# Graph layers over 25,000 edges: the last group's indirect transfers name 106 partitions instead of 128

## The chip, the core and the metric

The kernel is one program on one core of a Trainium2 chip. The metric is the device time of one launch in microseconds: the median of several executions. The core has a tensor engine (PE), a vector engine (DVE), a scalar engine (ACT), a GpSimd engine (POOL), and SyncE (SP), which here only issues transfers; transfers themselves run on 16 DMA engines.

## What is computed

The input is a table `x` of 50,000 nodes by 96 features, 25,000 edges (`src`, `dst`, sorted by `dst`), 17 attributes for each edge, and small weights. Four graph layers follow one another, each with a residual sum and a layer norm:

```python
x = _layernorm(x + _L0_gnn_ref(x, edge_index, edge_attr_17, ...))   # messages weighted by a small network
x = _layernorm(x + _L1_gnn_ref(x, edge_index))    # 10 times: out = spmm(out) * 0.9 + x * 0.1
x = _layernorm(x + _L2_gnn_ref(x, edge_index))    # 16 times: h = 0.9 * segment_sum(norm * h[row], col) + 0.1 * x
x = _layernorm(x + _L3_gnn_ref(x, edge_index, ...))  # two graph convolutions with weights and prelu
```

Each of the 10 + 16 + 2 steps after layer 0 gathers one row of 96 floats for every edge, adds the rows of edges that share a target node, and writes the sums for the next step.

## The kernel before, in words

**Tiles and groups.** The edges are laid out in 49 groups (`NGP`) of 512 slots: partition p of a group holds four consecutive slots (`U = 4`), and for each of the four there is one indirect transfer with one index for each partition, 128 rows of 384 bytes. So a pass over all edges is 49 x 4 = 196 indirect transfers, all issued by POOL. 48 groups (`GF`) are full. The last group holds 25,000 - 48 x 512 = 424 edges, which is exactly 106 partitions x 4; its partitions 106 to 127 are padding, with an index that is clamped into the table for a gather and out of bounds for a scatter.

**Stages.** The set-up (layer 0, histograms, ranks of the edges; not touched by the change) is followed by `passes()`, called four times: `power` (layer 1, 10 passes), `smooth` (layer 2, 16 passes), `conv1` and `conv2` (layer 3, one pass each). In a pass, for each group: POOL gathers four tiles into one of seven buffers `G` (line 1924), PE transposes them into a PSUM bank (1956), DVE scans along the sorted edges with a mask (2129), PE turns the result back (1976 or 1985), DVE combines it with the group's own rows (2154, 2169), and SP stores the result into the table of the next pass (2374). In `power` and `smooth` PE turns back group n two steps late: at the step of group 48, the last, it first turns back 46 and 47 and only then transposes 48 (`backs`, lines 1724 to 1728, and the loop at 2014).

**Order on POOL.** POOL issues in program order. It starts group g when group g-2 has landed (1920 to 1922) and the buffer is free. It starts a new pass when all stores of the pass before have landed (1912, 1913). Between the last gather of a pass and that wait other indirect transfers stand: in `power` 23 gathers of the nodes' own rows (1907; 12 in the last pass), in `smooth` a "lot" of two or three groups of finished rows that are scattered to the output (`send_lots`, 1881: 8 transfers in 10 passes, 12 in the five after them, 24 behind the last pass). In front of the `smooth` passes stand 196 gathers of own rows (1894). In `conv2` scatters of finished groups to the output (`send`, 1856) alternate with gathers, and the last twelve groups are scattered at the end. In 22 passes three of the four tiles of group 45 (`ROW_GROUP`) are fetched row by row by SP and ACT instead (1819); that is no part of the change.

**The last group.** It takes four indirect transfers in each place: 10 passes of `power`, the own rows of `power` (1907), the own rows of `smooth` (1894), 16 passes of `smooth`, the gathers of `conv1` and `conv2`, the last lot (1881, in `conv1`), and the last scatter (1856): 32 places, 128 transfers.

Of the kernel before, what the change touches and what calls it, by code (L numbers as in the profile page):

```python
# [19 lines left out]
N, E, D, ED = 50000, 25000, 96, 17  # L20
P = 128
U = 4
# [4 lines left out]
GF = E // GE  # L27
# [13 lines left out]
RG = 7  # L41
# [19 lines left out]
LOT_LOADED = {"smooth": tuple((p, 42) for p in range(15)) + ((15, 12), (15, 24)), "conv1": ((0, 8), (0, 20))}  # L61
ROW_GROUP, ROW_TILES, ROW_FROM, ROW_LOAD = NGP - 4, 3, 2, 8
ROWS = P * ROW_TILES
ROW_SHARES = {"sp": (0, 120, 3), "act": (120, ROWS, 7)}
EPS = 1e-5
GD = U * D
# [17 lines left out]
def slots_of(flat):  # L84

    return flat.rearrange("(g p u) -> p g u", p=P, u=U)


def by_group(x):
# [29 lines left out]
class Tail:  # L119


    def __init__(self, prog, s):
# [13 lines left out]
        def tmp(n, shape):  # L136
            return s.enter_context(nc.sbuf_tensor(f"tail_{n}", shape, fp32))

        self.X = tmp("x", [P, GD])
        wide = tmp("xt0", [D + 2, GE])  # L140
        prog.row_index = wide[D:D + 2, 0:ROWS].bitcast(i32)
        self.xt = [wide[0:D, :], tmp("xt1", [D, GE])[:, :]]
# [281 lines left out]
class Program:  # L424
# [50 lines left out]
    def build(self):  # L475
# [46 lines left out]
        self.outc = self.dram("outc", [TR, D])  # L522
        self.index_rows = self.dram("index_rows", [4, ROWS], i32)

# [773 lines left out]
    def prepare(self):  # L1298
# [4 lines left out]
        with ExitStack() as s:  # L1303
# [78 lines left out]
            def _(sp):  # L1382
# [14 lines left out]
                def order_out():  # L1397

                    sp.wait_ge(linked, 1)
                    with nc.allow_non_contiguous_dma(reason="four numbers of each partition"):  # L1400
                        sp.dma_start(slots_of(self.mask_s[1:TR + 1]), by_group(cont[:, :])).then_inc(self.order_masked, 16)
# [286 lines left out]
    def passes(self, name, mode):  # L1688
# [9 lines left out]
        first = {"power": self.x1t[:, :], "smooth": self.tab2[0:2 * TR, :], "conv1": self.x3t, "conv2": self.h1t}[mode]  # L1698
# [13 lines left out]
        T, XS = self.T, self.XS  # L1712
# [20 lines left out]
        def step(eng, p, g):  # L1733

            eng.wait_ge(stepped.sem, stepped.at + p * steps_of + g + 1)
# [13 lines left out]
        def tile(b, t):  # L1749
            return b[:, t % U * D:(t % U + 1) * D]  # L1750

        def stores_before(r, n):

            return len(range(r, n, RO))

        with ExitStack() as s:
            def tmp(n, shape, dt=fp32):
                return s.enter_context(nc.sbuf_tensor(f"{name}_{n}", shape, dt))

            G = [tmp(f"g{r}", [P, GD]) for r in range(RG)]  # L1760
# [19 lines left out]
            def by_rows(q):  # L1780

                return looped and 1 <= q // NGP < final and q % NGP == ROW_GROUP
# [20 lines left out]
            def fetch_rows(kind, eng, p, g):  # L1803

                begin, end, each = ROW_SHARES[kind]
                n = begin + (g - ROW_FROM) * each
# [24 lines left out]
            def own_chunk(t):  # L1831

                return t // OWN * -(-OWN // U) + t % OWN // U

            def own_count(k, end):

                return 16 * sum(own_chunk(t) < end and own_chunk(t) % RO == k % RO for t in range(NT))
# [11 lines left out]
            def send(pool, g):  # L1849

                pool.wait_ge(normed.sem, normed.at + g + 1)
                back = 1 if g < NGP - LAG else AHEAD_GROUPS
                if g >= back:
                    pool.wait_ge(sent[(g - back) % RO], 16 * U * len(range((g - back) % RO, g - back + 1, RO)))
                for t in range(g * U, (g + 1) * U):
                    nc.gpsimd.indirect_dma_start(  # L1856
                        out=self.out, out_offset=bass.IndirectOffsetOnAxis(ap=self.tgt_d[:, t:t + 1], axis=0),
                        in_=T[:, t * D:(t + 1) * D], in_offset=None, bounds_check=N - 1, oob_is_err=False,
                    ).then_inc(sent[g % RO], 16)

            def lot_groups(k):

                return sum(LOTS[:k]), sum(LOTS[:k + 1])
# [5 lines left out]
            def send_lots(pool, at):  # L1869

                for n, when in enumerate(lots_sent):
                    if when == at:
                        send_lot(pool, lots_before + n)

            def send_lot(pool, k):

                a, b = lot_groups(k)
                lot = self.lots[k % 2]
                pool.wait_ge(self.lot_in[k % 2], 16 * (k // 2 + 1))
                for t in range(a * U, b * U):  # L1880
                    nc.gpsimd.indirect_dma_start(
                        out=self.out, out_offset=bass.IndirectOffsetOnAxis(ap=self.tgt_s[:, t:t + 1], axis=0),
                        in_=lot[:, (t - a * U) * D:(t - a * U + 1) * D], in_offset=None,
                        bounds_check=N - 1, oob_is_err=False).then_inc(self.lot_out[k % 2], 16)

            @block.gpsimd
            def _(pool):
                self.start(pool)
                if smooth:
                    for g in range(NGP):  # L1890
                        if g >= AHEAD_GROUPS:
                            pool.wait_ge(self.fills(g - AHEAD_GROUPS), self.full(g - AHEAD_GROUPS))
                        for t in range(g * U, (g + 1) * U):
                            nc.gpsimd.indirect_dma_start(  # L1894
                                out=T[:, t * D:(t + 1) * D], out_offset=None, in_=first,
                                in_offset=bass.IndirectOffsetOnAxis(ap=self.own2[:, t:t + 1], axis=0),
                            ).then_inc(self.fills(g), 16)
                for p in range(K):
                    index = later[(p + 1) % 2] if p else index0
                    if p:  # L1900
                        if power:
                            for t in range((p - 1) * OWN, min(p * OWN, NT)):
                                n = own_chunk(t)
                                if n >= AHEAD_GROUPS and own_chunk(t - 1) != n:
                                    k = n - AHEAD_GROUPS
                                    pool.wait_ge(own_landed[k % RO], own_count(k, k + 1))
                                nc.gpsimd.indirect_dma_start(
                                    out=XS[:, t * D:(t + 1) * D], out_offset=None, in_=self.x1t,
                                    in_offset=bass.IndirectOffsetOnAxis(ap=self.own1[:, t:t + 1], axis=0),
                                ).then_inc(own_landed[own_chunk(t) % RO], 16)  # L1910
                        send_lots(pool, (p, 0))
                        for r in range(RO):
                            pool.wait_ge(stored[r].sem, stored[r].at + 16 * stores_before(r, p * NGP))
                    for g in range(NGP):
                        q = p * NGP + g
                        if q >= RG:
                            step(pool, (q - RG) // NGP, (q - RG) % NGP)
                        elif smooth:
                            pool.wait_ge(self.fills(own + q), self.full(own + q - RG))
                        back = 1 if out_rows and g > LAG else AHEAD_GROUPS + by_rows(q - 1)  # L1920
                        if q >= back:
                            pool.wait_ge(self.fills(own + q - back), self.full(own + q - back))
                        for t in range(g * U + ROW_TILES * by_rows(q), (g + 1) * U):
                            nc.gpsimd.indirect_dma_start(  # L1924
                                out=tile(G[q % RG], t), out_offset=None,
                                in_=tables[0:table_at + (2 - p % 2) * TR, :] if p else first,
                                in_offset=bass.IndirectOffsetOnAxis(ap=index[:, t:t + 1], axis=0),
                            ).then_inc(self.fills(own + q), 16)
                        if out_rows and g >= LAG:
                            send(pool, g - LAG)  # L1930
                send_lots(pool, (final, NGP))
                if out_rows:
                    for g in range(NGP - LAG, NGP):
                        send(pool, g)
                    for r in range(RO):
                        pool.wait_ge(sent[r], 16 * U * len(range(r, NGP, RO)))
                    for k in range(2):
                        pool.wait_ge(self.lot_out[k], 16 * U * sum(LOTS[k::2]))  # L1938

            @block.tensor  # L1940
            def _(pe):

                def turn(q):
# [4 lines left out]
                    if by_rows(q):  # L1948
                        for n, (begin, end, _) in ROW_SHARES.items():
                            pe.wait_ge(self.rows_in[n], 16 * (end - begin))  # L1950
# [488 lines left out]
```

## Time and profile before

| what | value |
|---|---|
| device time, three runs | 8951.67, 8959.77, 8965.37 us (median 8959.77) |
| span of the profiled execution, first to last instruction | 8950.4 us |
| median of the runs less that span | 9.4 us |
| POOL busy | 6658.3 us (74%), 7008 instructions, 6990 of them indirect transfers |
| PE / DVE / ACT busy | 5474.2 / 4879.1 / 1977.2 us |
| DMA | 939.53 MB, mean 105 GB/s |

The profile shows no device time of the profiled execution itself other than its span. The busy time of POOL for an indirect transfer is the time in which it makes the transfer's descriptors; that the rows have landed shows only in the instruction that waited for them. "issue" names idle time in which the engine waited for nothing that the profile shows. By stage, from the same trace: set-up to 1100 us, `power` to 3805, own rows of `smooth` to 4057, its passes and last lots to 8149, `conv1` to 8435, `conv2` to the end.

### The profile page before, as it was taken

To read this page: it belongs to the slowest core of one execution; us is meant where nothing else is said; L and a number is where in the kernel's file an instruction comes from. 1 tells how busy PE (TensorE), PEld (TensorE's weight loads), DVE (VectorE), ACT (ScalarE), POOL (GpSimd) and SP (SyncE) were. 2 spreads that over 40 slices of the span, in tenths; PEclk is the share of its full clock that TensorE was granted. 3 is DMA by queue.
4 is the path that set the end of the run, shared out by engine and by line. 5 is a ranking of instruction groups with operands and counts; after the bars stand their busy time and mean duration, and the time that the engine had idled before them with its cause. 6 is when DMAs were issued, how large, how long until landed. Compare 5 with 4: busy or idle time off the path is not lost. (4 is left out here: it accounts for less than half of the span.)

```text
span 8950.4 us, 111450 instructions
## 1 busy us (share of the span) xinstructions
PE 5474.2 (61%) x23642; PEld 4375.0 (49%) x23642; DVE 4879.1 (55%) x12173; ACT 1977.2 (22%) x5359; POOL 6658.3 (74%) x7008
## 2 busy tenths in 40 slices
PE   7566644444454443346777777877666667766643
PEld 6465533333333332225666666655555556555543
DVE  7687555555555556755555555544444444465444
ACT  2355631111111110633111111100000000056433
POOL 6677677777777777677777777777777777777777
PEclk9777755555555555557777777776777767665555
DMA  7664544444444443434444444443333334333311
GB/s 145 133 178 124 95 108 106 107 105 106 110 113 108 106 102 97 138 72 103 112 112 113 114 115 114 119 104 98 99 98 97 99 97 103 94 98 88 83 45 37
DMA packets 905581, 939.53 MB, mean 105 GB/s; under 512 B 380578, under 2 KB 796456, under 8 KB 904806
## 3 DMA queue, kind: packets, MB, share of 16 engines
q1 hardware_dynamic: 652430, 588.73, 22.0%
q0 software_dynamic: 223680, 320.10, 18.9%
q10 hardware_dynamic: 28794, 23.58, 0.9%
q8 instruction: 191, 3.13, 0.1%
q14 instruction: 486, 3.98, 0.1%
HBM read 560.22 MB, written 399.35 MB: 107 GB/s over the span
## 5 line engine op out<-in xcount | busy, mean ns | idle before, releaser
L1924 POOL DMA_INDIRECT l_g<-tab,l x2898 | 2737.2, 945 | 895.3 <-issue 830.4
L2129 DVE TENSOR_TENSOR_SCAN l_w<-l_m,l_w,bank 96x512 f32<-96x512 bf16 x1248 | 1591.9, 1276 | 2707.3 <-PE bank L1956 2690.3
L1956 PE MATMUL bank<-ident,l_g 128*96 128x128 f32 x5030 | 1171.1, 377 | 1887.8 <-DMA l_g<-tab,l 919.3
L1924 POOL DMA_INDIRECT l_g<-tab,XM x1740 | 1651.0, 949 | 530.7 <-issue 481.4
L1956 PEld LDWEIGHTS bank<-ident,l_g 128*96 128x96 f32 x5030 | 756.2, 172 | 2339.4 <-DMA l_g<-tab,l 1035.7
L1976 PEld LDWEIGHTS bank<-ident,l_w 96*128 96x128 f32 x6272 | 1602.7, 328 | 324.8 <-issue 252.4
L1976 PE MATMUL bank<-ident,l_w 96*128 96x96 f32 x6272 | 1507.1, 401 | 6.8 <-DVE l_w L2129 6.4
L1967 PE MATMUL bank<-XM,ident 128*128 128x384 f32 x1568 | 921.1, 681 | 0.0
L2046 ACT ACTIVATE T<-T,dinv_e 128x96 f32<-128x96 f32 x196 | 57.0, 361 | 1968.2 <-DVE T L2154 1966.2
L419 ACT ACTIVATE tail_y<-bank,tail_of,tail_sc 125x96 f32<-125x96 f32 (+1 forms) x596 | 208.7, 431 | 1236.1 <-DVE tail_of L410 1229.5
L308 PE MATMUL bank<-tail_xt,v 96*96 96x500 f32 (+1 forms) x298 | 275.3, 1025 | 316.0 <-ACT tail_xt L303 316.0
L2169 DVE TENSOR_TENSOR T<-bank,coef_d 128x384 f32<-128x384 f32 x735 | 410.0, 558 | 25.6
L1985 PE MATMUL bank<-ident,l_w 96*128 96x96 f32 x1960 | 403.6, 357 | 29.1 <-DVE l_w L2129 21.5
L2154 DVE TENSOR_TENSOR bank<-bank,T 128x384 f32<-128x384 f32 x735 | 394.6, 537 | 1.5 <-PE bank L1976 0.5
L1985 PEld LDWEIGHTS bank<-ident,l_w 96*128 96x128 f32 x1960 | 358.0, 227 | 46.4 <-DVE l_w L2129 33.7
L1967 PEld LDWEIGHTS bank<-XM,ident 128*128 128x128 f32 x1568 | 337.1, 265 | 4.0
L399 ACT ACTIVATE tail_sc<-tail_mv,eps_x 125x4 f32<-125x4 f32 (+1 forms) x149 | 44.3, 297 | 1278.2 <-DVE tail_mean L391 1278.2
L2129 DVE TENSOR_TENSOR_SCAN l_w<-l_m,bank 96x512 f32<-96x512 bf16 x26 | 31.6, 1217 | 442.2 <-PE bank L1956 427.9
L1894 POOL DMA_INDIRECT T<-tab,own x196 | 191.5, 977 | 90.8 <-issue 59.4
L1924 POOL DMA_INDIRECT l_g<-x1t,XM x196 | 185.5, 946 | 86.7 <-issue 80.8
L655 POOL DMA_INDIRECT T<-in_x_dram,src_i x196 | 189.6, 967 | 79.9 <-issue 55.2
L371 PE MATMUL bank<-ident,tail_up 96*125 96x96 f32 (+1 forms) x396 | 96.0, 392 | 233.4 <-DVE tail_up L361 233.4
(330 smaller groups left out, 9739.4 us busy)
## 6 DMA issues: line engine op xcount, KB each, us to landing
tab<-T SPq DMA_DIRECT2D x784, 192.0 KB
row_buffer<-tab ACTq DMA_DIRECT2D x5808, 0.4 KB
tab<-l_o SPq DMA_DIRECT2D x441, 192.0 KB
l_m<-mask_d SPq DMA_DIRECT2D x784, 96.0 KB
l_m<-mask_s SPq DMA_DIRECT2D x490, 96.0 KB
l_g<-tab,l POOLq DMA_INDIRECT x2898
row_buffer<-tab SPq DMA_DIRECT2D x2640, 0.4 KB
l_g<-tab,XM POOLq DMA_INDIRECT x1740
```

Of the source, the lines that this page charges most:

```text
L308: return self.nc.tensor.matmul(self.p.bank[5][0:D, 0:w], self.p.v1[0:D, :], self.xt[n % 2][:, 0:w], start=True, stop=True)
L419: last = self.nc.scalar.activation(self.Y[n % 2][0:R, c], self.p.bank[7][0:R, c], ACT.Identity, bias=self.of[n % 2][0:R, u:u + 1], scale=s ...
L655: nc.gpsimd.indirect_dma_start(out=T[:, t * D:(t + 1) * D], out_offset=None, in_=i["x"], in_offset=bass.IndirectOffsetOnAxis(ap=self.src_i ...
L1894: nc.gpsimd.indirect_dma_start(out=T[:, t * D:(t + 1) * D], out_offset=None, in_=first, in_offset=bass.IndirectOffsetOnAxis(ap=self.own2[: ...
L1924: nc.gpsimd.indirect_dma_start(out=tile(G[q % RG], t), out_offset=None, in_=tables[0:table_at + (2 - p % 2) * TR, :] if p else first, in_o ...
L1956: last = nc.tensor.transpose(a_bank(q)[0:D, u:GE:U], rows[:, u * D:(u + 1) * D], self.ident[:, :])
L1967: nc.tensor.matmul(b_bank(q)[:, 0:GD], self.ident[:, :], group(XS, q % NGP), start=True, stop=False, skip_group_check=True)
L1976: last = nc.tensor.matmul(b_bank(q)[:, u * D:(u + 1) * D], W[q % RW][:, u:GE:U], self.ident[0:D, 0:D], start=False, stop=True, skip_group_ ...
L1985: last = nc.tensor.transpose(b_bank(q)[:, u * D:(u + 1) * D], W[q % RW][:, u:GE:U], self.ident[0:D, 0:D])
L2129: v.tensor_tensor_scan(out=W[q % RW][:, :], data0=masks[q % RM][:, :], data1=a_bank(q)[0:D, :], initial=W[(q - 1) % RW][:, GE - 1:GE] if q ...
L2154: v.tensor_tensor(out=there if p == final else b, in0=b, in1=there, op=ALU.add).then_inc(summed.sem, 1)
L2169: v.tensor_tensor(out=by_row(o), in0=by_row(b), in1=by[:, at].unsqueeze(2).to_broadcast([P, U, D]), op=ALU.mult).then_inc(made.sem, 1)
```

## The change

A constant `IN_LAST = 106` and a function `used(t)` are added: for a tile t of the last group it gives partitions 0 to 105, for all others 0 to 127. The five places of `passes()` that issue indirect transfers take index, source and destination through it. The set-up's indirect transfers, the order of the work, the waits and all compute instructions stay as they were; buffers keep what they held before in partitions 106 to 127 of the last group.

```diff
--- before.py
+++ after.py
@@ -61,6 +61,7 @@
 LOT_LOADED = {"smooth": tuple((p, 42) for p in range(15)) + ((15, 12), (15, 24)), "conv1": ((0, 8), (0, 20))}
 ROW_GROUP, ROW_TILES, ROW_FROM, ROW_LOAD = NGP - 4, 3, 2, 8
 ROWS = P * ROW_TILES
+IN_LAST = 106
 ROW_SHARES = {"sp": (0, 120, 3), "act": (120, ROWS, 7)}
 EPS = 1e-5
 GD = U * D
@@ -84,6 +85,11 @@
 def slots_of(flat):
 
     return flat.rearrange("(g p u) -> p g u", p=P, u=U)
+
+
+def used(t):
+
+    return slice(0, P if t < GF * U else IN_LAST)
 
 
 def by_group(x):
@@ -1854,8 +1860,8 @@
                     pool.wait_ge(sent[(g - back) % RO], 16 * U * len(range((g - back) % RO, g - back + 1, RO)))
                 for t in range(g * U, (g + 1) * U):
                     nc.gpsimd.indirect_dma_start(
-                        out=self.out, out_offset=bass.IndirectOffsetOnAxis(ap=self.tgt_d[:, t:t + 1], axis=0),
-                        in_=T[:, t * D:(t + 1) * D], in_offset=None, bounds_check=N - 1, oob_is_err=False,
+                        out=self.out, out_offset=bass.IndirectOffsetOnAxis(ap=self.tgt_d[used(t), t:t + 1], axis=0),
+                        in_=T[used(t), t * D:(t + 1) * D], in_offset=None, bounds_check=N - 1, oob_is_err=False,
                     ).then_inc(sent[g % RO], 16)
 
             def lot_groups(k):
@@ -1879,8 +1885,8 @@
                 pool.wait_ge(self.lot_in[k % 2], 16 * (k // 2 + 1))
                 for t in range(a * U, b * U):
                     nc.gpsimd.indirect_dma_start(
-                        out=self.out, out_offset=bass.IndirectOffsetOnAxis(ap=self.tgt_s[:, t:t + 1], axis=0),
-                        in_=lot[:, (t - a * U) * D:(t - a * U + 1) * D], in_offset=None,
+                        out=self.out, out_offset=bass.IndirectOffsetOnAxis(ap=self.tgt_s[used(t), t:t + 1], axis=0),
+                        in_=lot[used(t), (t - a * U) * D:(t - a * U + 1) * D], in_offset=None,
                         bounds_check=N - 1, oob_is_err=False).then_inc(self.lot_out[k % 2], 16)
 
             @block.gpsimd
@@ -1892,8 +1898,8 @@
                             pool.wait_ge(self.fills(g - AHEAD_GROUPS), self.full(g - AHEAD_GROUPS))
                         for t in range(g * U, (g + 1) * U):
                             nc.gpsimd.indirect_dma_start(
-                                out=T[:, t * D:(t + 1) * D], out_offset=None, in_=first,
-                                in_offset=bass.IndirectOffsetOnAxis(ap=self.own2[:, t:t + 1], axis=0),
+                                out=T[used(t), t * D:(t + 1) * D], out_offset=None, in_=first,
+                                in_offset=bass.IndirectOffsetOnAxis(ap=self.own2[used(t), t:t + 1], axis=0),
                             ).then_inc(self.fills(g), 16)
                 for p in range(K):
                     index = later[(p + 1) % 2] if p else index0
@@ -1905,8 +1911,8 @@
                                     k = n - AHEAD_GROUPS
                                     pool.wait_ge(own_landed[k % RO], own_count(k, k + 1))
                                 nc.gpsimd.indirect_dma_start(
-                                    out=XS[:, t * D:(t + 1) * D], out_offset=None, in_=self.x1t,
-                                    in_offset=bass.IndirectOffsetOnAxis(ap=self.own1[:, t:t + 1], axis=0),
+                                    out=XS[used(t), t * D:(t + 1) * D], out_offset=None, in_=self.x1t,
+                                    in_offset=bass.IndirectOffsetOnAxis(ap=self.own1[used(t), t:t + 1], axis=0),
                                 ).then_inc(own_landed[own_chunk(t) % RO], 16)
                         send_lots(pool, (p, 0))
                         for r in range(RO):
@@ -1922,9 +1928,9 @@
                             pool.wait_ge(self.fills(own + q - back), self.full(own + q - back))
                         for t in range(g * U + ROW_TILES * by_rows(q), (g + 1) * U):
                             nc.gpsimd.indirect_dma_start(
-                                out=tile(G[q % RG], t), out_offset=None,
+                                out=tile(G[q % RG], t)[used(t), :], out_offset=None,
                                 in_=tables[0:table_at + (2 - p % 2) * TR, :] if p else first,
-                                in_offset=bass.IndirectOffsetOnAxis(ap=index[:, t:t + 1], axis=0),
+                                in_offset=bass.IndirectOffsetOnAxis(ap=index[used(t), t:t + 1], axis=0),
                             ).then_inc(self.fills(own + q), 16)
                         if out_rows and g >= LAG:
                             send(pool, g - LAG)
```

## Rows read from the trace of the kernel before

**Rows 1.** Busy time of each engine (first part of the page).

```profile
PE 5474.2 (61%) x23642; PEld 4375.0 (49%) x23642; DVE 4879.1 (55%) x12173; ACT 1977.2 (22%) x5359; POOL 6658.3 (74%) x7008
```

**Rows 2.** POOL's groups by line: busy us, mean ns, idle before, releasers.

```profile
L1924 POOL DMA_INDIRECT l_g<-tab,l x2898 | 2737.2, 945 | 895.3 <-issue 830.4 <-DMA l_g<-tab,l 52.8 <-DMA tab<-T 6.7
...
L1881 POOL DMA_INDIRECT out_dram<-XM,tgt_s x108 | 105.4, 976 | 32.9 <-issue 32.9
```

**Rows 3.** POOL's timeline, passes of `power`: start us, us, instruction, idle before.

```profile
1375.69 0.94 POOL L1907 DMA_INDIRECT XM<-x1t,XM  x1 [0.30 <-issue]
1376.94 0.94 POOL L1924 DMA_INDIRECT l_g<-tab,XM  x1 [0.30 <-issue]
...
3528.71 0.94 POOL L1907 DMA_INDIRECT XM<-x1t,XM  x1 [0.30 <-issue]
3529.96 0.94 POOL L1924 DMA_INDIRECT l_g<-tab,XM  x1 [0.30 <-issue]
```

**Rows 4.** POOL's timeline, passes of `smooth` behind a lot of 12 transfers.

```profile
6841.45 0.99 POOL L1924 DMA_INDIRECT l_g<-tab,l  x1 [0.30 <-issue]
...
7867.08 0.99 POOL L1924 DMA_INDIRECT l_g<-tab,l  x1 [0.30 <-issue]
```

**Rows 5.** POOL's timeline, passes of `smooth` behind a lot of 8 transfers.

```profile
4313.69 0.99 POOL L1924 DMA_INDIRECT l_g<-tab,l  x1 [2.16 <-DMA tab<-T]
...
5322.20 0.99 POOL L1924 DMA_INDIRECT l_g<-tab,l  x1 [0.30 <-issue]
...
6585.02 0.99 POOL L1924 DMA_INDIRECT l_g<-tab,l  x1 [2.25 <-DMA tab<-T]
```

**Rows 6.** Timeline of all engines around one such boundary.

```profile
5058.57 0.94 POOL L1924 DMA_INDIRECT l_g<-tab,l  x1 [0.30 <-issue]
...
5061.41 1.88 PE L1976 MATMUL bank<-ident,l_w 96*128 96x96 f32 x8
...
5063.42 0.64 PE L1956 MATMUL bank<-ident,l_g 128*96 128x128 f32 x4
...
5066.45 2.64 SPq L2374 DMA_DIRECT2D tab<-T  x3
...
5068.80 0.97 POOL L1881 DMA_INDIRECT out_dram<-lot,tgt_s  x1 [0.30 <-issue]
5070.90 0.99 POOL L1924 DMA_INDIRECT l_g<-tab,l  x1 [1.13 <-DMA tab<-T]
```

**Rows 7.** Timeline, the ends of `power` and of `smooth`.

```profile
3773.35 0.94 POOL L1924 DMA_INDIRECT l_g<-tab,XM  x1 [0.30 <-issue]
...
3776.47 1.06 PE L1956 MATMUL bank<-ident,l_g 128*96 128x128 f32 x4
...
3805.69 0.94 POOL L1894 DMA_INDIRECT T<-tab,own  x1 [31.40 <-POOLq L1756]
...
8154.90 0.99 POOL L1924 DMA_INDIRECT l3a_g<-x3t,l  x1 [5.22 <-POOLq L1756]
```

**Rows 8.** Timeline, the last gathers and the last scatter of `conv2`.

```profile
8872.45 0.95 POOL L1924 DMA_INDIRECT l3b_g<-h1t,l  x1 [0.30 <-issue]
...
8874.99 1.09 PE L1956 MATMUL bank<-ident,l3b_g 128*96 128x128 f32 x4 [4.26 <-DMA l3b_g<-h1t,l]
...
8939.61 0.97 POOL L1856 DMA_INDIRECT out_dram<-T,tgt_d  x1 [0.30 <-issue]
```

**Rows 9.** DMA queue of POOL's transfers: packets, MB, share of 16 engines.

```profile
q0 software_dynamic: 223680, 320.10, 18.9%
```

**Rows 10.** SP's issues: edge attributes (line 666), node tiles (258); ns min/median/max.

```profile
L666 SPq DMA_DIRECT2D XM<-in_edge_attr_dram x49: 254/328/1612, 15.2 to 257.5; - x49
...
257.54 0.25 SPq L666 DMA_DIRECT2D XM<-in_edge_attr_dram  x1
...
L258 SPq DMA_DIRECT2D tail_x<-x1t x100: 249/262/433, 1115.8 to 4004.7; - x100
L258 SPq DMA_DIRECT2D tail_x<-x3t x49: 354/355/442, 4067.2 to 5881.3; - x49
```

## The prediction

> **What bounds the kernel now.** I read the busy times first: POOL leads with 6658 us of the 8950 us span [rows 1]. That is 74%, and alone it would leave a quarter open. The groups of POOL's instructions close it: each gather takes 945 ns, each scatter 976, and the idle time before them is almost all "issue", some 0.30 us for each transfer [rows 2]. So a transfer costs 1.25 us of POOL's time, and 6990 of them (7008 instructions less 18 fills, iotas and selects) make about 8740 us. POOL issues without a stop nearly from one end to the other; what a change takes from a transfer there is worth that much of the total, wherever POOL does not wait at the next boundary between passes. So the third reading is the boundaries, one by one, in POOL's timeline:
>
> In `power` the 23 (last pass: 12) own-row gathers cover the boundary: the next pass starts 0.30 us behind them, first and last of nine boundaries alike [rows 3]. In `smooth` five boundaries behind lots of 12 are as tight [rows 4]. Of the ten behind lots of 8, eight wait for the stores of the old pass, the first 2.16 us, the last 2.25; the two others show 0.30 (one of them is the middle row) [rows 5].
>
> **What the waiting boundaries wait for.** The last gather's descriptors are ready at 5058.57 + 0.94 = 5059.51. In a quiet stretch the rows have landed 8874.99 - (8872.45 + 0.95) = 1.59 us later [rows 8], so here at about 5061.1. But PE turns back two earlier groups until 5061.41 + 1.88 = 5063.29 and takes up group 48 at 5063.42 [rows 6]. The last group lies ready for some 2.2 us. The chain to the stores at 5066.45 and to POOL's restart at 5070.90 hangs on PE and on the group before the last, not on the transfers that the change makes smaller. At these eight boundaries a shorter last group brings nothing, and one that lands up to 2 us later costs nothing.
>
> **The change, place by place.** It touches 32 places of four transfers, 128 in all. It removes no instruction and no wait; it makes 22 of 128 rows of each vanish.
>
> Places where POOL is never late behind them, so that a gain or loss on POOL counts in full: nine passes of `power`, own rows of `power` (12 transfers stand behind the old pass there and the boundary is still tight) [rows 3]; own rows of `smooth`, which run straight on into its first pass; five passes of `smooth` [rows 4] and its last, since 24 scatters follow and the next stage starts 5.22 us after POOL's last scatter [rows 7]; in `conv1` the gathers and the last lot; in `conv2` the gathers and the last scatters, after which nothing is left but their landing. That is 9 + 1 + 1 + 5 + 1 + 2 + 2 = 21 places, 84 transfers. The other 11 are the eight waiting boundaries, the last pass of `power`, behind which POOL idles 31.40 us while DVE and ACT finish [rows 7], and the two 8-lot boundaries at 0.30, where POOL arrives in the very moment; a gain there ends in a new wait, so I count them at nothing, and in the case of a loss I count them.
>
> *What 22 fewer rows save in making descriptors.* Every indirect transfer of the trace has 128 rows, so the price is bounded from both sides. If all of the 0.947 us (76 at 0.945, 8 at 0.976) went with the rows, 22/128 of it would go: 0.163 us, times 84 = 13.7 us. If the time is fixed, nothing goes. Rows that speak of a smaller number of partitions are SP's: the one load of 106 partitions took 254 ns where the median of 128-partition ones is 328, and loads of 125 partitions 262 where those of 128 take 355 [rows 10]. So something there goes with a count other than that of the partitions, since 3 of 128 can't make 93 ns. That is another engine's way of issuing, and I use it for a rival. Against a saving stands that POOL takes 0.99 us for the first gather after scatters, 0.05 us more than usual [rows 6]; if a change of size does the same, twice in a place, that is 21 x 0.10 = 2.1 us. I take the middle between fixed and proportional, 0.08 us for each transfer: 84 x 0.08 = 6.7 us.
>
> *Landing.* POOL's queue moved 223680 packets [rows 9], exactly 32 for each of 6990 transfers, which fits 16 engines with two each (one with 8 rows, one that signals). They took 18.9% of 16 x 8950 us, 27066 us, or 0.242 us for the pair and 0.030 us for a row. Seven rows on an engine instead of eight land 0.03 us earlier: nothing. PE, DVE, ACT and SP do what they did: zero. The stale data in 22 partitions travel through PE and DVE at the same cost as the clamped row did.
>
> *Sum.* 8950.4 - 6.7 = 8943.7 for the profiled span; with the 9.4 us between it and the median of the runs, 8953.1. I predict 8953.
>
> **A rule that bears on it.** The 32 packets above show each 128-row transfer on 16 engines. The Trainium skill, DMA: Bandwidth & Descriptors, section "Why a DMA increments its semaphore by 16 and not by 1", says that the number of engines is the largest one up to 16 that divides the slowest dimension of both sides, so that 106 = 2 x 53 would be put on two engines, with an exception for some direct copies of POOL, where each engine takes the partitions divided by 16, rounded up; it does not say which holds for indirect ones. SP's 125-partition loads, shorter by 93 ns, agree with fewer engines. By the exception the sum stays as above.
>
> **Rivals.**
>
> *A: shares of 53 rows, and POOL pays for the depth.* If 106 rows are dealt to two engines, each gets 53 in a line instead of 8. If POOL makes descriptors side by side for all engines, its time goes with the depth of a share. Half of 0.944 us by depth would be 0.059 us a step; 45 steps more are 2.7 us for each transfer. In 84 + 8 transfers that is 244 us, the eight waiting boundaries are pushed by some 9 us each (10.6 later, less slack of about 2), 72, and the end of `power` by 10: 326 us, 9286 us in all. If only a tenth of the time goes by depth, it is 0.5 us a transfer, some 50 us, 9010. If all did, it is twice the first. It decides from 0.2 us more for each transfer (92 x 0.2 = 18 us). For it: nothing in the trace shows POOL with anything but 128 rows, and 0.94 us for 8-deep shares leaves room for it. Against it: SP got faster, not slower, with 106 partitions.
>
> The two-engine rule of that section is what would set this case off; its sections give no duration by depth, so the price is the bound from the rows.
>
> *B: shares of 53 rows, and only the landing pays.* 53 x 0.030 = 1.6 us on an engine instead of 0.24: 1.36 us later. The eight waiting boundaries and the nine of `power` hide it (2.2 us there; 28 us of other transfers here). At the end of `power` the slack is 3776.47 - (3773.35 + 0.94 + 1.59) = 0.6 us [rows 7], so 0.8 us come through, and 1.4 at the very end behind the last scatter [rows 8]: +2.2 us, 8962 us with POOL unchanged.
>
> *C: the change does nothing.* Making descriptors has a fixed price; 8960 us.
>
> *D: POOL saves by the number of engines, as SP does.* 26% (262 against 355) of 0.947 is 0.246 us: 84 x 0.246 = 20.7 us, 8939 us. For it the rows of SP; against it that SP's descriptors are not made by POOL.
>
> **Chances.** A difference of 0.2%, 18 us, is about what can be told from no change here. My forecast (0.03 to 0.2 us saved for each transfer) 0.33; B and C together 0.25; D 0.15, and it alone is over the 18 us; A 0.27, all of it slower. So faster 0.15, same 0.58, slower 0.27. The likeliest case's own range is 8942 to 8958. The range to hold 8 in 10: downward to 0.35 us saved for each transfer, 84 x 0.35 = 29 us, 8930. Upward it must take in the lower part of A, up to 1.1 us for each of 92 transfers, 100 us: 9060; beyond it I leave about 0.15, below about 0.03.
>
> **What the profile after would show.** POOL's form of line 1924 should split or spread: four gathers before each lot at 0.85 to 0.90 us where all stood at 0.94. If they stand at 0.94, C; below 0.74, D; above 1.15, A. The packet count tells how the rows are dealt: 32 for each transfer with full spread. POOL's waits at the eight boundaries grow by what its last four gathers saved; if they shrink instead, the last group was on the chain and my reading of PE's slack is wrong. If the four gathers take longer, the waits vanish first. If the boundaries of `power` show more than 0.30 us, the stores are late and landing matters more than I hold. The forecast fails with any descriptor time outside 0.74 to 0.94 us.

## Result: the changed kernel is slower by 0.9%

The changed kernel takes 9038.05 us (median of five, 9033.52 to 9045.09) against 8951.67 for the one before in the same series (five, 8950.43 to 8965.37): a ratio of 1.0086 over all the runs (the two medians alone give 1.0096), 95% interval 1.0074 to 1.0097, so 66 to 87 us more. The forecast was 8953 and "the same"; the time is inside its range of 8930 to 9060 and on the other side of its point. The profiled execution took 9034.08 us with a span of 9032.2, 81.8 us more than the span before. The clock granted to TensorE is close in both, 0.655 before and 0.644 after.

Two lines of the changed kernel's page, against [rows 1, 9]: the busy times and POOL's DMA queue.

```profile
PE 5504.6 (61%) x23642; PEld 4385.3 (49%) x23642; DVE 4880.0 (54%) x12173; ACT 1977.3 (22%) x5359; POOL 6750.1 (75%) x7008
...
q0 software_dynamic: 231872, 319.47, 18.2%
```

POOL is busy 91.8 us longer with the same 7008 instructions, PE 30.3 us longer, DVE and ACT as before. (PE's part is not the loss: experiment 1 below has it 22.7 us longer too and loses nothing.) Fewer bytes moved and yet 8192 more packets: 64 more for each of the 128 changed transfers, 96 instead of 32.

The instructions of the gather line in the changed kernel (duration in ns: min, median, max), against the 945 ns of [rows 2]:

```profile
L1930 POOL DMA_INDIRECT l_g<-tab,l x2898: 941/947/1572, 4347.5 to 8183.8; - x194
L1930 POOL DMA_INDIRECT l_g<-tab,first_i x196: 943/947/1563, 4088.0 to 4334.2; - x196
```

The median hides what happened; the maximum has it. POOL's timeline at the end of the first pass of `smooth` shows a usual gather and the last group's four:

```profile
4327.32 0.94 POOL L1930 DMA_INDIRECT l_g<-tab,first_i  x1 [0.30 <-issue]
4328.57 1.56 POOL L1930 DMA_INDIRECT l_g<-tab,first_i  x1 [0.30 <-issue]
...
4334.16 1.55 POOL L1930 DMA_INDIRECT l_g<-tab,first_i  x1 [0.30 <-issue]
```

All 128 changed transfers stand at 1.55 to 1.60 us, gathers and scatters alike. They take 1.560 us in the mean against 0.951 before (by the median of the gathers, 0.616 us more), which makes 78 us. That is most of the loss; the other 13.7 of POOL's 91.8 us lie in the 6862 transfers that the change doesn't touch, and are taken up at the end. Where the loss lands is seen by stage, between the first instructions of each (`power`: 2705.2 us before, 2734.2 after; own rows, 251.2 and 254.5; passes and lots of `smooth`, 4098.0 and 4138.7; `conv1`, 285.5 and 290.9; `conv2`, 510.0 and 514.6).

The boundaries behind lots of 8, first and last, against [rows 5], and the ends of `power` and `smooth`, against [rows 7]:

```profile
4347.55 0.99 POOL L1930 DMA_INDIRECT l_g<-tab,l  x1 [1.54 <-DMA tab<-T]
...
6639.02 0.99 POOL L1930 DMA_INDIRECT l_g<-tab,l  x1 [0.50 <-DMA tab<-T]
```

```profile
3800.21 1.56 POOL L1930 DMA_INDIRECT l_g<-tab,XM  x1 [0.30 <-issue]
3804.27 1.09 PE L1962 MATMUL bank<-ident,l_g 128*96 128x128 f32 x4 [2.31 <-DMA l_g<-tab,XM]
...
3833.56 0.96 POOL L1900 DMA_INDIRECT T<-tab,own  x1 [31.79 <-POOLq L1762]
...
8226.74 0.99 POOL L1930 DMA_INDIRECT l3a_g<-x3t,l  x1 [5.23 <-POOLq L1762]
```

The reader is to see that the waits got shorter but did not go, although POOL came 2.46 us later to each: over the 0.30 us of an issue, the ten add up to 11.4 us before and 4.3 after. (The sum is what to compare. Which of the ten waits differs from trace to trace; in the traces of experiments 1, 5, 7 and 8 below, whose last group in `smooth` has 128 partitions or costs nearly the same, the sum is 9.9 to 12.0.) So something else moved too. It is the last group at PE, in the timeline of the same boundary as [rows 6]:

```profile
5098.85 1.56 POOL L1930 DMA_INDIRECT l_g<-tab,l  x1 [0.31 <-issue]
...
5102.97 0.64 PE L1962 MATMUL bank<-ident,l_g 128*96 128x128 f32 x4 [2.13 <-DMA l_g<-tab,l]
...
5106.01 2.72 SPq L2380 DMA_DIRECT2D tab<-T  x3
...
5111.00 0.99 POOL L1930 DMA_INDIRECT l_g<-tab,l  x1 [0.30 <-issue]
```

PE now waits 2.13 us for the last group, where it did not wait before, and takes it up 2.56 us after POOL made its last descriptor. In the kernel before it took it up 2.1 to 4.9 us after, without a wait of more than 0.13 us, at all 16 boundaries of `smooth`; now at 15 of them 2.5 to 2.8 us after, each time out of a wait for the transfer (the first waits for ACT's scaling). So the rows themselves land about 2.6 us after POOL. In quiet, at the last gather of `conv2`, it is 2.41 us (POOL ends at 8952.98 + 1.56, PE starts at 8956.95) instead of the 1.59 of [rows 8]. But the 1.59 is not what stood at these boundaries before. The traces also hold the updates of each transfer's semaphore, and the last of them tells the landing: at the 16 boundaries of `smooth` it came 1.5 to 3.9 us after POOL in the kernel before (mean 2.2) and 2.45 to 2.79 in the changed one (mean 2.6). At the boundary of [rows 6] it came 3.86 us after POOL, at 5063.37, and PE took the group up 0.05 us later.

### The profile page after: what moved, and what is told of

It reads as the page before. It is cut to its first block and busy times, and to the rows that moved or that the text cites. A ratio compares the mean times of both kernels' runs of the same rounds, so it can differ in the third digit from the quotient of the medians.

```text
span 9032.2 us, 111450 instructions
## 1 busy us (share of the span) xinstructions
PE 5504.6 (61%) x23642; PEld 4385.3 (49%) x23642; DVE 4880.0 (54%) x12173; ACT 1977.3 (22%) x5359; POOL 6750.1 (75%) x7008
## 5 line engine op out<-in xcount | busy, mean ns | idle before, releaser
L1930 POOL DMA_INDIRECT l_g<-tab,l x2898 | 2781.0, 960 | 888.7 <-issue 832.0
L1930 POOL DMA_INDIRECT l_g<-tab,XM x1740 | 1674.1, 962 | 530.9 <-issue 480.9
L1862 POOL DMA_INDIRECT out_dram<-T,tgt_d x196 | 195.6, 998 | 59.8 <-issue 49.1
```

Source lines behind the costliest of these rows:

```text
L1862: nc.gpsimd.indirect_dma_start(out=self.out, out_offset=bass.IndirectOffsetOnAxis(ap=self.tgt_d[used(t), t:t + 1], axis=0), in_=T[used(t), ...
L1930: nc.gpsimd.indirect_dma_start(out=tile(G[q % RG], t)[used(t), :], out_offset=None, in_=tables[0:table_at + (2 - p % 2) * TR, :] if p else ...
```

## Experiments

The theory after the first look: rows are dealt to as many engines as divide them, 106 to two; POOL's time for a transfer grows with the depth of a share. The rivals: any transfer short of 128 partitions, or any that is no multiple of 16, takes a slower path at a fixed price; or a price for each row. All kernels below are the changed one with one edit. Kernels of experiments 1 to 4 ran beside one series of the kernel before (median 8948.97 us, 21 runs), 5 to 8 beside another (8954.08, 11 runs).

**Experiment 1: 112 partitions.**

```diff
-IN_LAST = 106
+IN_LAST = 112
```

> The last group's transfers name 112 partitions (16 x 7) instead of 106. Theory 1 (POOL pays for the depth: rows are dealt to the largest number of engines up to 16 that divides them, and POOL's time is 0.944 us at 8 rows an engine and 1.56 at 53, so 0.0137 us for each row of depth): 16 engines, 7 deep, 0.93 us for each transfer, the time of the kernel before less 1 us, within 4 us of it; 32 packets for each transfer. Theory 2 (any transfer with fewer than 128 partitions takes a slower path at a fixed price): 1.56 us for each transfer, 9030 to 9045 us. Theory 3 (the loss is in the stale rows or the landing, not in making descriptors): 1.56 us stays unexplained and the time lies near 9038 too.

Measured: 8945.74 us, ratio 0.9997 (0.9988 to 1.0006). The first of the last four gathers of the same pass, from POOL's timeline (as in the experiments below):

```profile
4292.04 0.93 POOL L1930 DMA_INDIRECT l_g<-tab,first_i  x1 [0.30 <-issue]
```

22 rows less cost 0.62 us, 16 rows less save 0.01. The whole loss is gone with six more partitions, and stale rows, masks and compute are the same: "any transfer short of 128" falls, and so does a loss that isn't in POOL's transfers. As a version it beats the changed kernel and ties with the one before.

**Experiment 2: 107 partitions**, a prime number (`IN_LAST = 107`).

> 107 partitions, a prime number: one row more than 106. Theory 1 (depth): one engine, 107 deep: 0.944 + 99 x 0.0137 = 2.30 us for each transfer; 128 x 1.36 = 174 us over the kernel before, less 11 us of waits that are taken up, 9115 to 9140 us. Theory 2 (a fixed price for what is no multiple of 16): 1.56 us as with 106, about 9038 us. Theory 3b (a price for each row on the slower path): 1.57 us, 9040 us.

Measured: 9130.68 us in one run, with

```profile
4364.84 2.28 POOL L1930 DMA_INDIRECT l_g<-tab,first_i  x1 [0.30 <-issue]
```

and in its queue

```profile
q0 software_dynamic: 242112, 319.96, 18.2%
```

One row more than 106 takes 0.72 us more. A fixed price and a price for each row both fall; depth had said 2.30. One part of the expectation missed: 11 us of wait were to be taken up, but over the 0.30 us of an issue the ten boundaries now wait 16.6 us in all. One of them, with PE's wait for the last group, whose last gather starts at 5148.45 and takes 2.28 us:

```profile
5154.56 1.09 PE L1962 MATMUL bank<-ident,l_g 128*96 128x128 f32 x4 [5.37 <-DMA l_g<-tab,l]
...
5162.61 0.99 POOL L1930 DMA_INDIRECT l_g<-tab,l  x1 [1.60 <-DMA tab<-T]
```

The last group lands 3.7 us after POOL there in the mean, 1.1 us later than with 106 partitions; ten times that is 11 us, most of the growth from 4.3 to 16.6. So the landing of the last group is on the chain to POOL's restart. Packets: 242112 less the 223680 of [rows 9] are 18432, 144 more for each of 128 transfers: 176 instead of 32.

**Experiment 3: 53 partitions** (`IN_LAST = 53`), the depth of 106 with half the rows.

> 53 partitions: half the rows of 106 at the same depth of 53 (one engine instead of two). It leaves out the edges in partitions 53 to 105 of the last group, from layer 1 on. Theory 1 (depth alone): 1.56 us for each transfer, the same as with 106, 9030 to 9045 us. Theory 3b (a price for each row): about half of the added 0.62 us, 1.25 us, 9000 us. If the number of engines counts beside the depth, it lies between.

Measured: 9024.76 us in one run (span 9023.0, 9.2 below the changed kernel's).

```profile
4328.18 1.56 POOL L1930 DMA_INDIRECT l_g<-tab,first_i  x1 [0.30 <-issue]
```

The same 1.56 us and the same 96 packets, for one engine with rows as for two. The time lies 5 us under the expected range of 9030 to 9045; between the two traces the usual 128-row gathers differ too (median 944 ns here, 947 in the changed kernel), and the 6862 unchanged transfers together take 12.0 us less here. Why one execution has 947 and all others 944 or 945 is open.

**Experiment 4: 114 partitions**, 6 engines with 19 rows (`IN_LAST = 114`).

> 114 partitions = 6 x 19. Theory 1 (depth): 6 engines, 19 deep, 0.944 + 11 x 0.0137 = 1.09 us for each transfer; 128 x 0.15 = 19 us, less what the waiting boundaries take up (64 transfers, up to 9 us): 8955 to 8975 us. Theory 2 (a fixed price for what is no multiple of 16): 1.56 us, about 9038 us.

Measured: 8965.70 us, ratio 1.0021 (1.0012 to 1.0030), that is +11 to +27 us.

```profile
4303.83 1.12 POOL L1930 DMA_INDIRECT l_g<-tab,first_i  x1 [0.30 <-issue]
```

On the expected line, 0.03 us above it. This trace has 227 transfers between 1.06 and 1.5 us, of which 128 are the changed ones; the other 99 are about as many as in the other kernels (78 to 98).

**Experiment 5: only layer 1** (44 transfers). `used` got a second argument, and false gives all partitions:

```diff
-def used(t):
+def used(t, narrow=True):
...
-                                out=tile(G[q % RG], t)[used(t), :], out_offset=None,
+                                out=tile(G[q % RG], t)[used(t, power), :], out_offset=None,
```

> 106 partitions only in layer 1: the last group of its 10 passes and its own rows, 44 of the 128 transfers; 128 partitions everywhere else. Its passes begin behind 12 to 23 other transfers, so a late landing is covered and only POOL's time counts: 44 x 0.62 = 27 us over the kernel before, 8972 to 8980 us. If landing (about 1 us later by the quiet boundary of conv2) also came through at its boundaries, it would be 37 us or more. If the loss had come from elsewhere (layer 2, the final scatters), nothing.

Measured: 8984.31 us, ratio 1.0033 (1.0020 to 1.0045), +18 to +40 us (4 us above the expected range, which was reckoned from a lower time of the kernel before); by stage `power` takes 2730.7 us, +25.5, own rows 250.9 and the rest as before. POOL's time alone says 27. So a later landing costs nothing behind 12 to 23 other transfers; behind the last pass, where there are none, POOL's wait is 31.97 us instead of the 31.40 of [rows 7].

**Experiment 6: only the passes of layer 2** (64 transfers; `used(t, smooth)` in the same place, all partitions elsewhere).

> 106 partitions only in the gathers of the 16 passes of layer 2, 64 of the 128 transfers. POOL's time alone: 64 x 0.62 = 39 us. Theory 1a (the waits at the ten boundaries behind lots of 8 take up part of it, as in the changed kernel, where they fell from 11.4 us over the 0.30 of an issue to 4.3): 39 - 7 = 32 us over the kernel before, 8977 to 8985 us. As the prediction had it (the last group has 2.2 us of slack at PE, so the chain to the stores isn't moved and the waits are used up first): 39 - 11 = 28 us, with no wait left over. Theory 1b (the added landing time comes through at all 16): 39 + 13 us. PE's wait for the last group at these boundaries, which was none before, should be about 2 us under 1a.

Measured: 8989.00 us, ratio 1.0039 (1.0026 to 1.0051), +23 to +46 us. That is above the expected 8977 to 8985 us, which was reckoned from a lower time of the kernel before, and the interval holds the prediction's 28 as well as theory 1a's 32. The stage is sharper than the total: its passes take 4130.4 us, +32.4, while `power` (2704.1) and the others stay; in experiments 1, 5 and 8, where the stage had no loss to show, it takes 4098.8 to 4099.5. The waits over 0.30 us add up to 5.3 us, where the prediction's way would have left none. The same boundary:

```profile
5077.47 1.55 POOL L1930 DMA_INDIRECT l_g<-tab,l  x1 [0.30 <-issue]
...
5081.82 1.09 PE L1962 MATMUL bank<-ident,l_g 128*96 128x128 f32 x4 [1.51 <-DMA l_g<-tab,l]
...
5089.84 0.99 POOL L1930 DMA_INDIRECT l_g<-tab,l  x1 [0.54 <-DMA tab<-T]
```

39.4 us from POOL less the 6.1 by which the waits fell make 33.3: theory 1a. PE waits for the last group 0.7 to 3.0 us, and what POOL's later arrival could have hidden in its waits is partly given back.

**Experiment 7: 16 partitions** (`IN_LAST = 16`), one row for each engine.

> 16 partitions, one row for each of 16 engines. It leaves out most of the last group's edges (partitions 16 to 105) from layer 1 on. Theory 1 (depth): 0.944 - 7 x 0.0137 = 0.85 us for each transfer, so a fixed price of 0.83 us and, for all 128 transfers, -12 us, of which the waiting boundaries keep some 5: 8940 us. If the time below 8 rows an engine goes with the rows instead (16 of 128), it is 0.1 to 0.3 us and the time 8880 us or less.

Measured: 8944.45 us in one run.

```profile
4297.33 0.85 POOL L1930 DMA_INDIRECT l_g<-tab,first_i  x1 [0.30 <-issue]
```

112 rows fewer save 0.10 us. Carried on to a depth of nothing, the line leaves 0.83 us of a transfer as its fixed part (an estimate). A price by the rows alone, which would have given 0.1 to 0.3 us, falls.

**Experiment 8: 120 partitions** (`IN_LAST = 120`), 15 engines with 8 rows.

> 120 partitions = 15 x 8: the depth of 128, one engine fewer, and no multiple of 16. Theory 1 (depth alone): 0.944 us for each transfer, no difference from the kernel before (within 10 us in a single time), 32 packets for each transfer. Theory 2b (what is no multiple of 16 pays a fixed part beside the depth, as 1.12 us at 19 deep instead of the 1.09 expected could mean): 0.96 to 1.0 us.

Measured: 8959.50 us in one run, no difference that one run can tell.

```profile
4302.51 0.99 POOL L1930 DMA_INDIRECT l_g<-tab,first_i  x1 [0.30 <-issue]
```

Depth alone, the first of the two theories, misses by 0.04 us; the second holds: a number that is no multiple of 16, so that not all engines get rows, pays about that beside the depth.

Together (median of the last group's gathers, by rows and the depth that the rule of division gives):

Packets are worked out as in experiment 2.

| partitions | engines x depth | POOL, us | packets each |
|---|---|---|---|
| 16 | 16 x 1 | 0.85 | 32 |
| 112 | 16 x 7 | 0.93 | 32 |
| 128 | 16 x 8 | 0.94 | 32 |
| 120 | 15 x 8 | 0.98 | 32 |
| 114 | 6 x 19 | 1.12 | 48 |
| 53 | 1 x 53 | 1.56 | 96 |
| 106 | 2 x 53 | 1.56 | 96 |
| 107 | 1 x 107 | 2.28 | 176 |

0.944 us + 0.035 where it is no multiple of 16 + 0.013 for each row of depth over 8 gives 1.12, 1.56 and 2.27. The time follows the depth column and neither the first nor the number of engines with rows. The count of engines in the table is worked out by that rule (the Trainium skill, DMA: Bandwidth & Descriptors, "Why a DMA increments its semaphore by 16 and not by 1"); the runs agree with it in eight of eight sizes and rule out the exception that the page names for some direct copies, since 7 rows on each of 16 engines would have cost 106 partitions what they cost 112. Four of the sizes tell the two apart, 53, 106, 107 and 114.

The traces show the dealing itself, in the sizes of POOL's packets. Experiment 6, against the kernel before, has for each of its 64 changed transfers 8 packets of 4224 bytes (11 rows of 384) and 2 of 3456 (9 rows): two shares of 4 x 11 + 9 = 53 rows. Beside them stand 56 packets of 44 bytes and 14 of 36: fourteen shares of 4 x 11 + 9 = 53 entries of 4 bytes. The other 16 packets have 4 bytes each, one signal for each engine. So the fourteen engines without rows get as many entries as the two that have them. The count of such shares is 15 with 53 and 107 partitions, 10 with 114, 1 with 120 and 0 with 112 and 16, as the table has it. Since every engine gets a share of the full depth, "by depth" and "by the number of entries for all 16 engines" are the same thing in all these runs; which of the two costs POOL the time isn't separated.

## Why the prediction was wrong

**What bounds the kernel: right.** POOL's time counted in full at the tight places: in experiment 5 `power` +25.5 us where 44 x 0.616 is 27.1; in the changed kernel `conv1` +5.4 and `conv2` +4.6 where two places each make 4.9.

**What 22 fewer rows save: this step failed.** I put the price between fixed and proportional to the rows and took the middle, 0.08 us saved, a term of -6.7 us. Both bounds assumed that fewer rows can't cost more, for which no row spoke: POOL had 128 rows in all its transfers, as I wrote under rival A. Measured: +0.616 us for each, 78 us in all, because the time goes by the depth of a share, 53 instead of 8. That the time lies inside the range is owed to the width given for rival A, not to this sum. A gain and a loss were both open there; I let the loss in only as rival A at 0.27, below a saving for which no row spoke either, at 0.33.

**Rival A: the right one, and mis-sized at its middle.** I took half of 0.944 us to go with depth; it is 0.10 us of it (8 x 0.013), about the "tenth" of that paragraph, which gave 0.53 us for each transfer, some 50 us, and 9010 us. The span grew by 81.8. The difference is the 0.62 us measured against 0.53 (8 us over 92 transfers); the eight waiting boundaries, 8 x 2.46 less the 7.1 us taken up = 12.6 us, and the end of `power`, 2.5 us, which the sum for that size left out; and about 10 us of the remainder below. Shares of 53 rows, priced by depth, were what happened, and I gave them 0.27.

**The landing, rival B: right in kind, and the slack beside it was misread.** 1.36 us later was worked out. By the semaphore updates the last gather landed 0.8 to 0.9 us later in quiet places (end of `power` 1.57 and 2.46 us after POOL, `conv2` 1.54 and 2.37), the last scatter 1.40 us later (1.15 and 2.55). But from POOL's last scatter to the end of the kernel it is 9.77 us before and 8.57 after, so the 1.4 us put there did not come through. The slack of 2.2 us at PE was read with the quiet place's 1.59 us, and at that very boundary the rows landed 3.86 us after POOL: there was no slack. At the eight waiting boundaries it was 0.05 to 3.1 us, in the mean 1.7. The change spends it twice: POOL is 2.46 us later and the rows land 0.4 us later still in the mean, so the last group becomes the chain to the stores, and the boundaries gave up 7.1 us of wait instead of 11.4.

**Rival D fell**: SP's shorter issue with 125 partitions (262 against 355 ns) does not carry over to descriptors made by POOL, where 2 engines take longer than 16. **What the profile should show** was a good list: the gathers above 1.15 us, packets off 32, and shrinking waits each named A or the chain.

A remainder: 78 us of POOL's time less 7 absorbed is 71; the span grew by 81.8. The 6862 unchanged transfers took 13.7 us more in that trace than in the one before, the 3 ns for each gather; in the traces of the eight experiments they take between 2.8 us less and 6.1 us more. Experiment 3 comes without it: 78 us less 6.2 of wait, and its span grew by 72.6. Where the 13.7 us come from isn't settled.

## What to carry to other kernels

The number of partitions of an indirect transfer is worth its divisors: round a partial tile up to a multiple of 16 (106 to 112, or leave 128) rather than name only the rows in use. Before a size is changed from the one that all rows of a profile have, treat its price as open in both directions; a smaller transfer isn't a lower bound of the cost. And where a change delays an engine and the data behind it, add both before calling a slack enough, and take the landing from the place itself: between a quiet place and a boundary it differed by up to 2.3 us here.

## What the runs showed of the hardware

An indirect transfer on POOL has a fixed price of 0.83 us (estimated from the line through the depths), beside 0.30 us of issue, so its rows hardly count: 16 rows 0.85, 128 rows 0.94. Entries are made for all 16 engines at the depth of the longest share: 53 partitions on one engine and 106 on two both move 96 packets, and the engines without rows get entries of 4 bytes, 53 each. Those are 70 packets for each changed transfer, which is why the changed kernel has 8950 more packets under 512 bytes. Dealt to two engines, the last group landed 2.4 to 2.8 us after its descriptors; dealt to sixteen, 1.5 to 1.7 us in quiet places and up to 3.9 us between other transfers.
